# Edge routing of a graph layer: three one-hot columns on ScalarE, five record planes for six, and weight rows written during counting

## The reference

```python
h = layernorm(x)                                     # 3125 x 256
msg = silu(concat(h[src], h[dst], edge_weight) @ mW1 + mb1)
msg = silu(layer_norm(msg) @ mW2 + mb2)
agg = segment_sum(msg, src, 3125)                    # src is not sorted
x = x + h + (silu(concat(h, agg) @ uW1 + ub1) @ uW2 + ub2)
x = x + ffn(layernorm(x))                            # top-k gated, on all nodes
```

## Time and profile before

| what | us |
|---|---|
| runs shown | 2132.20, 2132.21, 2133.16 (median 2132.21) |
| the profiled execution | 2126.56 |
| its span in the profile | 2124.8 |
| counting | about 16 to 153 |
| routing and tables | about 160 to 402 |
| edge loop | about 415 to 1840 |
| PE, DVE, ACT, POOL busy in the whole span | 1848.7, 1847.5, 1501.9, 1483.0 |

### The profile page before, as it was taken

One profiled execution on the slowest core, in us unless ns is written; L12 is line 12 of the kernel. 1 busy time (PEld: TensorE's weight loads), 2 busy tenths in 40 slices (PEclk: granted clock), 3 DMA queues, 4 the chain that ended last, 5 costly groups with the idle time before them and its releaser, 6 DMA issues. The chain is left out here.

```text
span 2124.8 us, 46537 instructions
## 1 busy us (share of the span) xinstructions
PE 1848.7 (87%) x11277; PEld 1603.5 (75%) x11278; DVE 1847.5 (87%) x4642; ACT 1501.9 (71%) x3084; POOL 1483.0 (70%) x1393
## 2 busy tenths in 40 slices
PE   3554665259999999999999999999999999799996
PEld 1333554258999999999999989999999899577775
DVE  5788999568999999999999999999999999655895
ACT  2322332149999999999999999999999999323322
POOL 8767888487888888888888888888888886503000
PEclk9996887579999999999999999999999999899998
DMA  4000000245333333333333333433333335101001
GB/s 133 1 0 12 30 30 25 90 121 160 104 104 101 107 100 107 103 103 104 104 104 101 106 101 107 102 105 104 104 104 101 106 102 65 43 1 21 10 1 61
DMA packets 109820, 169.16 MB, mean 80 GB/s; under 512 B 42785, under 2 KB 79571, under 8 KB 109517
## 3 DMA queue, kind: packets, MB, share of 16 engines
q0 software_dynamic: 43168, 114.55, 21.1%
q1 hardware_dynamic: 61086, 48.90, 7.5%
q10 hardware_dynamic: 5516, 5.08, 0.8%
HBM read 156.30 MB, written 11.74 MB: 79 GB/s over the span
## 5 line engine op out<-in xcount | busy, mean ns | idle before, releaser
L961 POOL DMA_INDIRECT g_rows<-b_table,idx_ring x816 | 849.4, 1041 | 237.2 <-issue 212.3
L1097 PE MATMUL ps<-w2g,nT 128*128 128x256 f32 x3432 | 815.4, 381 | 1.2 <-ACT rec L997 1.2
L1097 PEld LDWEIGHTS ps<-w2g,nT 128*128 128x128 f32 x3432 | 620.8, 191 | 68.6 <-ACT rec L997 1.4
L1004 ACT ACTIVATE normed<-act,rec 128x255 f32<-128x255 f32 x858 | 467.6, 596 | 88.0 <-DVE rec L1162 83.5
L1069 PE MATMUL psH<-a_sb,ohT 128*128 x1716 | 345.3, 324 | 43.2 <-DVE ohT L1176 39.4
L1069 PEld LDWEIGHTS psH<-a_sb,ohT 128*128 128x128 f32 x1716 | 257.9, 192 | 97.7 <-issue 74.9
L1196 DVE BATCH_NORM_STATS2 rec<-act 128x6 f32<-128x256 f32 x858 | 316.6, 409 | 1.9 <-ACT act L1018 1.9
L1202 DVE TENSOR_TENSOR low<-rec,high 128x512 fp32r<-128x512 f32 x429 | 301.5, 703 | 1.1 <-ACT high L1010 1.1
L1190 DVE TENSOR_TENSOR g_rows<-psH,g_rows 128x512 f32<-128x512 f32 x429 | 292.5, 682 | 10.0 <-DMA g_rows<-b_table,rec 8.3
L1018 ACT ACTIVATE act<-g_rows 128x512 f32<-128x512 f32 x429 | 267.5, 624 | 19.7 <-DVE g_rows L1190 19.5
L1010 ACT ACTIVATE high<-rec 128x512 fp32r<-128x512 f32 x429 | 266.7, 622 | 0.2
(11 more groups left out here) (206 smaller groups left out, 2397.3 us busy)
## 6 DMA issues: line engine op xcount, KB each, us to landing
loc_rows<-loc_d SPq DMA_DIRECT2D x143, 187.5 KB
g_rows<-b_table,idx_ring POOLq DMA_INDIRECT x816
h_sb<-in_x SPq DMA_DIRECT2D x1, 3125.0 KB
b_table<-b_out SPq DMA_DIRECT2D x25, 125.0 KB
x_all<-in_x ACTq DMA_DIRECT2D x1, 3125.0 KB
out<-x_all SPq DMA_DIRECT2D x5, 625.0 KB
ohT<-ew_d SPq DMA_DIRECT2D x143, 9.0 KB
idx_ring<-rec SPq DMA_DIRECT2D x136, 3.0 KB
```

What stands on the lines that cost most here:

```text
L961: pool.indirect_dma_start(g_rows[:, j, n, :], None, b_table[:, :], bass.IndirectOffsetOnAxis(ap=which, axis=0)).then_inc(s_gather[j], 16)
L1004: ins = nc.scalar.activation(normed[:, (j - 10) % 2, n, 0:D - 1], act1[:, (j - 10) % RING, n, 0:D - 1], ACT.Identity, scale=rstd_e[:, g % ...
L1097: mm = pe.matmul(ps2[:, (j - 13) % 2, n, :], nT[:, (j - 13) % 2, n, q, :], w2g[:, q, :], start=(q == 0), stop=(q == 1))
```

## The change

ACT makes three of the 13 one-hot matrices (`ora`, a ring of three), in two steps: `offsets(s)` writes (r - iota)^2 for three columns with Square, and `columns(s)` turns these 128 x 384 values into relu(1 - off), which is one where r equals iota and zero elsewhere. DVE makes seven in place of ten. `vals` has five planes: plane 4 is the destination plus 0x3000, written by DVE as a 16-bit integer in iteration 8 of counting and carried as the bit pattern of a bf16. The `cast` and `plane` steps for the destination go. 17 of the 25 `weight_rows` (blocks 8 to 24, whose memory holds none of the edge arrays) are written by ACT in iterations 6 to 22 of counting.

```diff
-PLANES = 6
+PLANES = 5
+ACOLS = 3
+ARING = 3
+DCOLS = COLS - PCOLS - ACOLS
+FREE_BLOCK = -(-5 * EC // (2 * D))
@@ ACT, counting: cast(i)
-                        nc.scalar.activation(g3[:, :], dst_i[:, :], ACT.Copy).then_inc(s_cast, 1)
-                        act.wait_ge(s_cast, 2)
-                        nc.scalar.activation(g4[:, :], g3[:, :], ACT.Copy, scale=1.0 / 64,
-                                             bias=-31.5 / 64).then_inc(s_cast, 1)
...
-                    elif i == 10:
-                        act.wait_ge(s_planes, 3)
-                        nc.scalar.activation(vals[:, :, 4], g4[:, :], ACT.Copy).then_inc(s_cast, 1)
@@ ACT, end of each counting iteration i
+                    if i == 6:
+                        act.wait_ge(s_parts, 2)
+                    if 6 <= i < 6 + BLOCKS - FREE_BLOCK:
+                        weight_rows(FREE_BLOCK + i - 6)
@@ ACT, routing
+                def offsets(s):
+                    if s:
+                        act.wait_ge(s_ora, s)
+                    for k in range(ACOLS):
+                        c = s * COLS + DCOLS + k
+                        ins = nc.scalar.activation(off[:, k, :], iota_n[:, :], ACT.Square, scale=-1.0, bias=r_all[:, c:c + 1])
+                    ins.then_inc(s_off, 1)
+
+                def columns(s):
+                    act.wait_ge(s_off, s + 1)
+                    if s >= ARING:
+                        act.wait_ge(s_win, s - ARING + 1)
+                    nc.scalar.activation(ora[:, s % ARING, :, :], off[:, :, :], ACT.Relu, scale=-1.0,
+                                         bias=onesf[:, 0:1]).then_inc(s_ora, 1)
...
+                for s in range(ARING - 1):
+                    offsets(s)
+                    columns(s)
                 for s in range(SUPERS):
                     b = s // 2
+                    if s + ARING - 1 < SUPERS:
+                        offsets(s + ARING - 1)
                     if s % 2 == 0 and b < BLOCKS:
                         turned(b)
                         if b + 2 < BLOCKS:
                             normal(b + 2)
-                        weight_rows(b)
+                        if b < FREE_BLOCK:
+                            weight_rows(b)
                     if s % 2 == 1 and b < BLOCKS:
                         ab_rows(b)
                     window(s)
+                    if s + ARING - 1 < SUPERS:
+                        columns(s + ARING - 1)
@@ POOL, counting: plane(i)
-                    elif i == 5:
-                        pool.wait_ge(s_cast, 3)
-                        pool.tensor_scalar(g4[:, :], g4[:, :], MAGIC, None, ALU.add).then_inc(s_planes, 1)
...
-                    elif i == 18:
-                        pool.wait_ge(s_planes, 5)
-                        pool.tensor_tensor(vals[:, :, 5], g3[:, :], g4[:, :], ALU.add).then_inc(s_planes, 1)
@@ PE
+                    pe.wait_ge(s_ora, s + 1)
...
-                    for k, plane in enumerate((0, 4, 5)):
+                    for k, plane in enumerate((0, 4)):
@@ DVE, counting
+                    if i == 8:
+                        dve.wait_ge(s_edges, 96)
+                        link(V.tensor_scalar(vals[:, :, 4].bitcast(I16), dst_i[:, :], PATTERN, None, ALU.add))
@@ DVE, routing and after
                     V.tensor_tensor(or_[:, s % 2, :, :],
-                                    r_all[:, mine].unsqueeze(2).broadcast_to([P, COLS - PCOLS, P]),
-                                    iota_v.unsqueeze(1).broadcast_to([P, COLS - PCOLS, P]), ALU.is_equal)
+                                    r_all[:, mine].unsqueeze(2).broadcast_to([P, DCOLS, P]),
+                                    iota_v.unsqueeze(1).broadcast_to([P, DCOLS, P]), ALU.is_equal)
...
-                    link(V.tensor_copy(low_part[:, g * P:g * P + n], psR[:, g % 2, 2, 0:n]))
-                    V.scalar_tensor_tensor(out=idx_all[:, g * P:g * P + n], in0=psR[:, g % 2, 1, 0:n], scalar=64.0,
-                                           in1=low_part[:, g * P:g * P + n], op0=ALU.mult, op1=ALU.add)
+                    V.tensor_scalar(idx_all[:, g * P:g * P + n], psR_bits[:, g % 2, 1, 0:n], -PATTERN, 0, ALU.add, ALU.max)
```

More of the change, by code:

```diff
@@ L48 @@
 MAGIC_W, MAGIC_P = MAGIC * WIN, MAGIC * 2 * P
+PATTERN = 0x3000
+DCOLS = COLS - PCOLS - ACOLS
+FREE_BLOCK = -(-5 * EC // (2 * D))
 def build(nc, io):
@@ L122, in build @@
             g2 = a_mem[:, 4 * EC:5 * EC].bitcast(F32)
-            g3 = a_mem[:, 5 * EC:6 * EC].bitcast(F32)
-            g4 = a_mem[:, 6 * EC:7 * EC].bitcast(F32)
             f1 = x_all[:, 0 * EC:1 * EC]
@@ L138, in build @@
             ew_c = x_all[:, TG * P // 2:TG * P // 2 + TG * 3 * P].rearrange("p (g n r) -> p g n r", g=TG, n=3)
-            low_part = x_all[:, TG * P // 2 + TG * 3 * P:TG * P // 2 + TG * 3 * P + TG * P]
             lists = agg_all[:, 0:(4 * BLOCKS + 1) * SUPERS].rearrange("p (b s) -> p b s", s=SUPERS)
@@ L155, in build @@
             tb_i = sb("tb_i", [P, PG], I32)
-            or_ = sb("or_", [P, 2, COLS - PCOLS, P], BF16)
+            or_ = sb("or_", [P, 2, DCOLS, P], BF16)
+            off = sb("off", [P, ACOLS, P], BF16)
+            ora = sb("ora", [P, ARING, ACOLS, P], BF16)
             orp = [half[:, k * PCOLS * P // 2:(k + 1) * PCOLS * P // 2].bitcast(BF16).rearrange("p (t r) -> p t r", t=PCOLS)
@@ L182, in build @@
             psK = ctx.enter_context(nc.psum_tensor("psK", [P, 6, 512], F32))
-            psR = psK[:, 0:2, 0:3 * P // 2].bitcast(BF16).rearrange("p g (n t) -> p g n t", n=3)
+            psR = psK[:, 0:2, 0:P].bitcast(BF16).rearrange("p g (n t) -> p g n t", n=2)
+            psR_bits = psK[:, 0:2, 0:P].bitcast(I16).rearrange("p g (n t) -> p g n t", n=2)
             iota_v = psV[:, 0:P]
@@ L239, in build @@
             s_orp = sem("s_orp")
+            s_off = sem("s_off")
+            s_ora = sem("s_ora")
             s_places = sem("s_places")
@@ L318, in cast, with weight_rows, weight_rows_done @@
                         nc.scalar.activation(vals[:, :, 2], g1[:, :], ACT.Copy).then_inc(s_cast, 1)
-                    elif i == 10:
-                        act.wait_ge(s_planes, 3)
-                        nc.scalar.activation(vals[:, :, 4], g4[:, :], ACT.Copy).then_inc(s_cast, 1)
                     elif i == 14:
-                        act.wait_ge(s_planes, 4)
+                        act.wait_ge(s_planes, 2)
                         nc.scalar.activation(vals[:, :, 3], g2[:, :], ACT.Copy).then_inc(s_cast, 1)
+                def weight_rows(b):
+                    nc.scalar.activation(a_sb[WP:P, b, :, :], w_parts[WP:P, :, :], ACT.Copy).then_inc(s_wrows, 1)
+                def weight_rows_done(b):
+                    return b - FREE_BLOCK + 1 if b >= FREE_BLOCK else BLOCKS - FREE_BLOCK + b + 1
                 def tallies(i):
@@ L357, in normal @@
                                          bias=neg[:, b:b + 1]).then_inc(s_h, 1)
-                def weight_rows(b):
-                    nc.scalar.activation(a_sb[WP:P, b, :, :], w_parts[WP:P, :, :], ACT.Copy).then_inc(s_wrows, 1)
                 def ab_rows(b):
                     act.wait_ge(s_ab, b + 1)
-                    act.wait_ge(s_wrows, b + 1)
+                    act.wait_ge(s_wrows, weight_rows_done(b))
                     nc.scalar.activation(a_sb[0:NB, b, 0, :], psA[0:NB, 0:D], ACT.Copy).then_inc(s_hi, 1)
@@ L386, in _ @@
                 normal(1)
-                act.wait_ge(s_parts, 2)
-                act.wait_ge(s_planes, 7)
-                act.wait_ge(s_cast, 6)
+                def offsets(s):
[11 more added lines that the diff above has]
+                                         bias=onesf[:, 0:1]).then_inc(s_ora, 1)
+                act.wait_ge(s_planes, 3)
+                act.wait_ge(s_cast, 3)
+                act.wait_ge(s_pool, 18)
+                act.wait_ge(s_places, 1)
+                for s in range(ARING - 1):
+                    offsets(s)
+                    columns(s)
                 for s in range(SUPERS):
                     b = s // 2
+                    if s + ARING - 1 < SUPERS:
+                        offsets(s + ARING - 1)
                     if s % 2 == 0 and b < BLOCKS:
@@ L420, in _ @@
                 pool.memset(src_i[:, TAIL:EC], -1).then_inc(s_pads, 1)
-                pool.memset(dst_i[:, TAIL:EC], 0).then_inc(s_pads, 1)
+                pool.memset(dst_i[:, TAIL:EC], -PATTERN).then_inc(s_pads, 1)
                 pool.memset(ew_f[:, TAIL:EC], 0.0).then_inc(s_pads, 1)
@@ L467, in plane @@
                         pool.tensor_tensor(g1[:, :], ew_f[:, :], vals[:, :, 1], ALU.subtract).then_inc(s_planes, 1)
-                    elif i == 5:
-                        pool.wait_ge(s_cast, 3)
-                        pool.tensor_scalar(g4[:, :], g4[:, :], MAGIC, None, ALU.add).then_inc(s_planes, 1)
-                    elif i == 7:
-                        pool.wait_ge(s_planes, 2)
-                        pool.tensor_scalar(g4[:, :], g4[:, :], -MAGIC, None, ALU.add).then_inc(s_planes, 1)
```

(27 more changed lines are left out.)

## The result

The change makes the kernel slower: 2202.65 us, median of 4 runs (2198.22 to 2206.12), against 2132.2 (2131.85 to 2133.16); ratio 1.0335, 95% interval 1.0323 to 1.0347.

The account below looks back on a forecast made before the run. DVE bounds routing now; the ACT-PE loop would bind after the change at 9.0 us a pair. Routing +45.6, counting -1.4, last supers -0.5, end -0.3 gave +43.4: 2170 profiled, 2176 us median, range 2145 to 2195.

Parts of the forecast that it names:

- ACT's wait for `route`: Routing loop, listed under what would show the forecast right: this wait of ACT shrinks; no size given.
- ACT's 4.36: ACT's part of the ACT-PE routing loop: 1.27 + 3.04 + 0.05 = 4.36 us a pair.
- Which clock: Routing: nearly every table begins at 1.2 GHz; 9.0 us a pair, 21 x (9.0 - 6.83) = +45.6.
- rows 7: Profile rows of the old routing loop where the clock begins at 1.2 GHz: PE's part 4.84 us.
- the start: Before block 3: first table some 3.7 us late, absorbed by DVE's extra work: 0, bounds 0 and +5.
- the second rival: Routing: clock stays low through tables and route, or new steps dearer; 10.2 us a pair, 2201 us; 12%.
- Rows 8: Profile rows of the old routing loop where the clock stays low throughout: PE's part 5.88 us.
- the first rival: Routing: the ACT-PE loop binds but PE stays at full clock; +14, 2146 us; 15%.
- Counting: Counting stage: four POOL steps go, saving 3.4 us; new DVE write adds 2.0; together -1.4 us.
- The last twelve supers and the end: Last 12 supers, paced by DVE or POOL, -0.5 us; after routing, fewer transposes and DVE copies, -0.3.
- POOL as the bound: Routing: rival that POOL's 6.1 us a pair becomes the bound; -17.5, 2114 us; 8%.

Follow-up runs that it names:

- The filler run: The change plus eight unused 512-column PE matmuls behind each odd route from s = 11 to 47: 2150.54 us, ratio 1.0091.
- the order swapped: The change with ACT's offsets(s+2) placed behind turned/normal/weight_rows and ab_rows instead of ahead of them; same instructions: 2143.22 us, ratio 1.0062.

## Why the prediction was wrong, and where it was right

**The bound and the place: right.** "Between the end of route(2b) and the next hT, ACT now runs, in order: window, Relu, Squares ..." is the timeline above, line by line, 4.24 us for a forecast 4.36. Undoing the columns, or placing them behind hT, takes the whole loss away. DVE fell to 54% busy, where near 60% was said. One sign was stated wrongly: ACT's wait for `route` did not shrink. It is one wait of 5.5 us a pair now and was 78.1 us over 18.3 pairs, 4.3 a pair, before (215 to 340 us). ACT's 4.36 holds a small slip as well: three Squares at 0.39 with 0.11 of overlap each are 0.84 and not 0.87; they hold ACT for 0.89.

**The term that failed is "Which clock".** The text took 9.0 us a pair, "eight pairs in nine like rows 7", where the clock begins low and rises during the tables. It begins low and stays low to the end of the even route in every steady pair: 5.96 us, 10.18 a pair. 21 x 1.18 = 24.8 us. In the profiles the miss is 79.6 - 43.4 = 36.2 us: 24.8 is this term, 5.9 the start, 3.6 the spread of the rest, and the small terms make up what is left. By the medians it is 26.7, since the two profiled executions lie on opposite sides of their medians. The row was there; I gave it 12% as the second rival, whose 2201 us is the measured time to 2 us. Its pair of 10.2 us was right; that the total fits so well is in part luck, as it too had nothing for the start, and between the profiles it gives 69.2 us for the measured 79.6. What misled me was to take the nearest steady pair, as the price of a low clock. That pair followed two short waits of PE, 0.61 us ahead of its tables and this one ahead of the odd route:

```profile
231.62 0.60 PE L647 MATMUL psK<-oqv,or_ 128*128 128x96 bf16 x10 [2.15 <-DVE oqv L784]
```

Rows 8 followed a wait of 14.0 us with only 0.7 us of work behind it, nearer to the new kernel, where PE idles 3.8 us in one piece in every pair. The filler run shows that the rest is the clock: with it up, the loop is 7.40, the 7.6 of the first rival.

**The range.** It ended at pairs of 9.9 us; a mechanism priced at 10.2 with 12% was left outside together with the faster side. Its lower end, 2145, served a case that needed a full clock against the text's own argument.

**The start: missed.** The text had 0, bounds 0 and +5; it is +5.9. Ahead of the first hT stand nine Squares, with the loop's own first three, and two Relus; the first tables start at 171.60 for 169.39. The next two pairs take 10.4 and 10.3 us for 7.1 and 11.6 before, so the tables of block 1 come 5.4 us late and those of block 3 4.8, counting's 1.1 already taken off. DVE's extra work, which was to absorb the delay, absorbed little of it.

**Counting: right.** -1.4 forecast, -1.1 measured. The new DVE write took 3.02 us for 2.84. The last twelve supers and the end: -0.8 forecast, +1.0 in the profile for the part up to the records, small either way.

**The rules named.** The Trainium skill's page ScalarE: Activation LUTs ("What ACT_TABLE_LOAD costs") gives, as an estimate from its formula, 0.386 and 0.60 us for the two new forms; the trace has 0.391 and 0.612. The Trainium skill's rule to put relu and multiply on VectorE (the same page, "Rules for kernel authors") did not decide: with the same Squares and Relus on ACT, behind hT, the kernel is faster than before. Per element the rows even went the other way, 1.15 ns on DVE against 0.84 on ACT. The place was wrong, not the engine, though in the right place the engine wins only the 2.5 us named above.

**The other side.** POOL as the bound came true only in part once the loop was cleared. Pairs of 6.34 lie near its 6.1, but with a column moved off POOL they stayed at 6.28; of the 11 us which that gave, 8.6 were won in the last twelve supers. The prediction did not ask about this, because it took POOL's floor as given.

## What to carry to other kernels

An engine that is 38% busy can still have no room in the one place where the new work is put: before moving work to an idle engine, write down what that engine does between the last result it receives and the next one another engine waits for, and put the work after that hand-over, not ahead of it. When a change makes TensorE wait longer, price its next work from a row that follows a similar wait, and not from a row that follows shorter ones: here a wait of 3.8 us put all of it at 1.2 GHz. And when a loop is cleared, ask at once for the next bound, since there most of the gain may lie: here 0.4% from the change with its columns in the right place, of which 0.2% come without any column on ACT, and 0.8% more from POOL's column and the block list. Whether those 0.8% need ACT's columns was not tried.

## What the runs showed of the hardware that was not expected

- In the change, PE was busy 63% of each pair and still was granted 0.67 of its clock; in the kernel before, a pair busy 57% ran at 1.00, and the next began low. The idle pieces ahead of the tables differ, 3.8 us in one stretch against 2.4 and 0.6 us apart. That the length of the wait decides is not shown: with the order swapped, tables behind the same wait of 2.69 us began at either level.

```profile
292.07 2.07 PE L654 MATMUL psK<-wij,hT 128*125 128x256 f32 x4 [2.69 <-ACT hT L381]
...
299.72 1.13 PE L654 MATMUL psK<-wij,hT 128*125 128x256 f32 x4 [2.69 <-ACT hT L381]
```

- 1.9 us of matmuls without any use, in a gap of 3.4 us, made the kernel 52 us faster. With the clock held up the pairs were regular to 0.01 us (7.40 and 7.41), as they are in the change with it low in every pair (10.20 and 10.21 from block 11 on); in the runs between, where it changes from pair to pair, they were not.
- A step of the loop may cost more than its length: 1 us of ACT moved off the loop shortened pairs by 2.4 us.
- The 2 KB transfer in 4-byte pieces holds up POOL's next scatter wherever it is put: by 8.05 us at s = 52 and by 8.2 and 7.8 at s = 12, with and without the change; in the run with the columns behind hT by 5.5. Whether the pieces themselves cause it was not tried.
